# A fused Mamba-2 and quantised-FFN block on one core: new hand-written orders of VectorE, ScalarE, GpSimd and SyncE in the 16-chunk scan

## The reference, cut to what matters

```
x = x + 0.5 * ffn(layernorm(x))          # ffn: 4-bit weights dequantised, 512x512, plus LoRA and bias
h = layernorm(x)
a = h + mamba2(rmsnorm(h, ln1_w))        # 4 heads of 128, state 128x128 each, chunks of 128 tokens
a = a + down(silu(gate(rmsnorm(a, ln2_w))) * up(...))        # inner size 1792
x = x + a
x = x + 0.5 * ffn(layernorm(x))
```

```
z, xs, Bs, Cs, dt = split(h @ w_in.T)         # 512, 128, 128, 512, 4 columns
xs, Bs, Cs = silu(conv4(xs, Bs, Cs));  dt = softplus(dt + dt_bias)
Y  = (tril(exp(cs_q - cs_k)) * (C B^T)) (dt x) + exp(cs) C S_prev + D x
S  = exp(cs_last) S_prev + sum(dec_end * B * dt x)
out = (Y * silu(z)) @ w_out.T
```

## Time and profile before

| what | value |
|---|---|
| median of 3 runs | 782.08 us (781.28 to 782.09) |
| profiled execution, its own time | 783.73 us |
| its span in the trace | 782.0 us |
| PE / DVE / ACT / POOL busy | 96% / 82% / 59% / 45% of the span |
| mean granted PE clock | 0.985 of full |

### The profile page before, as it was taken

One profiled execution on the slowest core, in us unless ns is written; L12 is line 12 of the kernel. 1 busy time (PEld: TensorE's weight loads), 2 busy tenths in 40 slices (PEclk: granted clock), 3 DMA queues, 4 the chain that ended last, 5 costly groups with the idle time before them and its releaser, 6 DMA issues.

```text
span 782.0 us, 10656 instructions
## 1 busy us (share of the span) xinstructions
PE 748.5 (96%) x3424; PEld 364.4 (47%) x3424; DVE 642.9 (82%) x1245; ACT 458.2 (59%) x895; POOL 352.8 (45%) x403
## 2 busy tenths in 40 slices
PE   8999997999899789799999999999999999999998
PEld 3444554555455445354444444444444444444444
DVE  7799998778768887996799988878779779657994
ACT  4868877587765666554536555645645555535451
POOL 5631646565453358866614125124224224223574
PEclk9999999999899899999999999999999999999999
DMA  8934645654421121524060554544544643444464
GB/s 299 186 74 80 167 95 105 138 114 90 83 64 41 41 55 40 128 48 95 14 148 15 103 123 79 140 81 81 139 84 75 148 82 68 76 81 66 105 178 142
DMA packets 98790, 77.67 MB, mean 99 GB/s; under 512 B 65600, under 2 KB 73088, under 8 KB 98736
## 3 DMA queue, kind: packets, MB, share of 16 engines
q0 software_dynamic: 17280, 31.46, 22.6%
q1 hardware_dynamic: 78592, 41.01, 19.9%
q10 hardware_dynamic: 2864, 4.52, 2.4%
HBM read 24.77 MB, written 5.54 MB: 39 GB/s over the span
## 4 chain that ended last, share of the span: by engine, by line
PE 63%; DVE 21%; ACT 8%; issue 4%; DMA 2%; POOL 2%; ACTq 0%; SPq 0%; DVEq 0%; POOLq 0%
PE PS L2123 57%; DVE raw L1578 3%; DVE stage L1578 2%; PE PS L2261 1%; DVE w_in L1682 1%; DVE state L1560 1%; DVE st L1399 1%; DMA x_t<-hb 1%; PE PS L2229 1%; PE PS L2253 1%; DVE h2n_p L1490 1%; DVE xs L1498 1%; ACT xds L922 1%; ACT pre L972 1%; DVE S L1534 1%
## 5 line engine op out<-in xcount | busy, mean ns | idle before, releaser
L2123 PE MATMUL PS<-h,w_in 128*128 128x512 f16 x480 | 111.5, 388 | 0.6 <-DMA h<-hn_p 0.5
L2123 PE MATMUL PS<-h,x_t 128*128 128x512 f16 x408 | 94.0, 379 | 1.7 <-DVE pre L1948 1.6
L773 POOL DMA_DIRECT2D xs<-x x42 | 36.4, 866 | 94.0 <-ACT x L1263 93.1
L2123 PEld LDWEIGHTS PS<-h,w_in 128*128 128x128 f16 x480 | 47.3, 100 | 65.4 <-issue 15.7
L2123 PE MATMUL PS<-n_T,stage 128*128 128x512 f16 x288 | 71.5, 379 | 0.0
L1263 ACT ACTIVATE x<-PS,d_d 128x512 f32<-128x512 f32 x59 | 40.3, 683 | 39.5 <-PE PS L2123 38.6
L2123 PEld LDWEIGHTS PS<-h,x_t 128*128 128x128 f16 x408 | 39.4, 98 | 50.2 <-issue 2.6
L576 POOL TENSOR_TENSOR r<-mv,mhalf 128x1 f32<-128x1 f32 (+1 forms) x32 | 29.4, 920 | 69.3 <-DVE mv L1403 53.0
L2123 PE MATMUL PS<-pre,stage 128*128 128x512 f16 x192 | 49.3, 379 | 0.0
L1233 ACT ACTIVATE xds<-tm,dgh 128x512 f32<-128x512 f32 x24 | 17.3, 722 | 53.3 <-DVE tm L2047 53.3
L2123 PEld LDWEIGHTS PS<-n_T,stage 128*128 128x128 f16 x288 | 28.2, 98 | 34.0 <-ACT x L1263 0.3
(11 more groups left out here) (352 smaller groups left out, 1910.6 us busy)
## 6 DMA issues: line engine op xcount, KB each, us to landing
xs<-x POOLq DMA_DIRECT2D x58, 256.0 KB, 3.3
xs<-n POOLq DMA_DIRECT2D x21, 256.0 KB, 3.3
xl<-x POOLq DMA_DIRECT2D x17, 256.0 KB, 3.3
x_t<-x_in SPq DMA_DIRECT2D x16, 256.0 KB, 3.1
x_t<-hb POOLq DMA_DIRECT2D x16, 256.0 KB, 3.8
out<-x_t SPq DMA_DIRECT2D x15, 256.0 KB, 2.3
raw_gu<-gate_t SPq DMA_DIRECT2D x7, 512.0 KB, 4.5
raw_gu<-up_t SPq DMA_DIRECT2D x7, 512.0 KB, 6.4
```

The lines of the kernel that those rows point to most:

```text
L773: po.dma_start(end_row(c), d_tmps[d % 3], accum_op=ALU.add).then_inc(s_acc[d % 3], 16)
L2123: ins = pe.matmul(out_, lhs(a, b, k), rhs(a, b, k), start=first and n == 0, stop=last and n == len(todo) - 1)
```

## The change

Four things are changed.

1. In steps 0 to 7 the order inside `step(c)` is altered. On POOL, `low_y(c)` goes ahead of `ln1_chain` and `scan_c` at j = 2. On ACT, `conv` is issued ahead of `hi1` at j = 1, and the second slot is copied out ahead of `square` at all j but 2. On DVE, the first two `cut_decay` go ahead of `lo1`.
2. Steps 8 to 15 leave `step` and are written out by hand for DVE, ACT and POOL (`late_steps`). On DVE, `gate_y`, `advance`, `weights` and `scan1` come ahead of taps, `silu`, `lo2`, weight cuts and low parts of sums; on POOL the sums lie between the scan's operations; on ACT `high_y` and `scan_decay` come early.
3. `low_y` of chunks 11 to 15 is on DVE (before: 11, 12, 13, 15; chunk 14 was on POOL). For these chunks `gate_y` writes y in place into PSUM bank B_YT, ACT's `high_y` and DVE's `low_y` read it from there, and PE's `s2_diag(c)` waits for the low part of chunk c-1 too.
4. On SP `load_pair` is cut into `load_gu` and `load_d`. `load_gu(1)` now waits for the first weight cut alone and is issued in step 14, `load_d(1)` is issued after the transpose of chunk 13's h2 (which waits for `lo2(13)` on DVE).

PE's own list is unchanged but for the wait.

Where y of a chunk lives, and `gate_y` on DVE:

```
-        LO_DVE = (11, 12, 13, 15)
+        LO_DVE = range(2 * CH + 3, NCH)
         def y_of(c):
-            return szs[(c // CH) % 2][:, :, cols], y_lo[(c // CH) % 2][:, :, cols]
+            sz = szs[(c // CH) % 2][:, :, cols]
+            return sz, heads(B_YT) if c in LO_DVE else sz, y_lo[(c // CH) % 2][:, :, cols]
...
             def gate_y(c, j):
-                y = szs[(c // CH) % 2][:, :, cols]
-                ve.scalar_tensor_tensor(y, heads(B_YT), d_ih[:, :], y, ALU.mult, ALU.mult).then_inc(e_y, 1)
+                sz, y, _ = y_of(c)
+                ve.scalar_tensor_tensor(y, heads(B_YT), d_ih[:, :], sz, ALU.mult, ALU.mult).then_inc(e_y, 1)
```

PE's added wait in `s2_diag`, and SP's loads within the loop over c:

```
+                if c - 1 in LO_DVE:
+                    pe.wait_ge(e_y_lo, c)
...
+                if c == 3 * CH + 2:
+                    load_gu(1)
...
                 if c > 3 * CH:
                     t2(c - 1)
+                if c == 3 * CH + 2:
+                    load_d(1)
```

`step` of POOL, and of ACT:

```
             def step(c):
                 a = c + 2 * CH
...
+                if c % CH == 2:
+                    low_y(c)
+                ln1_chain(a, a % CH)
+                scan_c(c + 1, (c + 1) % CH)
+                if c % CH != 2:
+                    low_y(c)
...
+                if j in (1, 2):
                     slot_a(i + 1, SLOTS[j][0])
```

`late_steps` of DVE, chunks 10 and 14 of the eight:

```
+                c = 2 * CH + 2
+                gate_y(c, 2)
+                advance(c, 2)
+                bound_row(0)
+                taps(3, 4, 12)
+                for k in range(15, 18):
+                    softplus(3, k)
+                weights(c + 1, 3)
+                scan1(c + 1, 3)
+                silu(3, 4)
+                scale_read(0)
+                lo2(c - 1)
...
+                c = 3 * CH + 2
+                gate_y(c, 2)
+                advance(c, 2)
+                low_y(c)
+                scan1(c + 1, 3)
+                lo2(c - 1)
+                bound_g(1, 0)
+                gate_up(0, 2)
+                residual2(c, 2)
```

More of the change, by code:

```diff
@@ new lines, in step, with late_steps @@
+                if j != 2:
+                    residual2(c, j)
+                slot_b(i + 1, SLOTS[j][0])
+            def late_steps():
+                c = 2 * CH
+                silu_z(2, 3)
+                gate_y(c, 0)
+                advance(c, 0)
+                lo2(c - 1)
+                weights(c + 1, 1)
+                scan1(c + 1, 1)
+                maximum_gu(0)
+                taps(3, 0)
+                softplus(3, 0)
+                softplus(3, 1)
+                softplus(3, 2)
+                residual2(c, 0)
+                silu(3, 0)
+                c = 2 * CH + 1
+                taps(3, 1, 3)
+                gate_y(c, 1)
+                advance(c, 1)
+                weights(c + 1, 2)
+                scan1(c + 1, 2)
+                taps(3, 2, 6)
+                silu(3, 1)
+                silu(3, 2)
+                lo2(c - 1)
+                maximum_gu(1).then_inc(e_max, 1)
+                taps(3, 3, 9)
+                residual2(c, 1)
+                silu(3, 3)
+                c = 2 * CH + 2
+                gate_y(c, 2)
[5 more added lines that the diff above has]
+                weights(c + 1, 3)
+                scan1(c + 1, 3)
+                silu(3, 4)
+                scale_read(0)
+                lo2(c - 1)
+                for k in range(4):
+                    cut_decay(3, k)
+                residual2(c, 2)
+                taps(3, 5)
+                silu(3, 5)
+                c = 2 * CH + 3
+                gate_y(c, 3)
+                scales(0)
+                descale(0)
+                silu_z(3, 0)
+                low_y(c)
+                silu_z(3, 1)
+                advance(c, 3)
+                weights(c + 1, 0)
+                scan1(c + 1, 0)
+                cut_a()
+                lo2(c - 1)
+                silu_z(3, 2)
+                residual2(c, 3)
+                silu_z(3, 3)
+                c = 3 * CH
+                gate_y(c, 0)
+                advance(c, 0)
+                low_y(c)
+                weights(c + 1, 1)
+                scan1(c + 1, 1)
+                lo2(c - 1)
+                t_los(0, 0, 1)
+                gate_up(0, 0)
+                residual2(c, 0)
+                t_los(0, 2)
+                cut_b_gu()
+                c = 3 * CH + 1
+                gate_y(c, 1)
+                advance(c, 1)
+                low_y(c)
+                weights(c + 1, 2)
+                scan1(c + 1, 2)
+                gate_lo(0, 0)
+                gate_up(0, 1)
+                residual2(c, 1)
+                lo2(c - 1)
+                dn_lo(0)
+                t_los(0, 3)
+                gate_lo(0, 1)
+                c = 3 * CH + 2
+                gate_y(c, 2)
+                advance(c, 2)
+                low_y(c)
+                scan1(c + 1, 3)
+                lo2(c - 1)
+                bound_g(1, 0)
+                gate_up(0, 2)
+                residual2(c, 2)
+                bound_g(1, 1)
+                gate_lo(0, 2)
+                bounds(1)
+                c = 3 * CH + 3
+                gate_y(c, 3)
+                low_y(c)
+                t_los(1, 0, 1)
+                lo2(c - 1)
+                gate_up(0, 3)
+                residual2(c, 3)
+                t_los(1, 2, 3)
+                gate_lo(0, 3)
+                bound_row(1)
@@ L1956, in _ @@
             prologue()
[L1957 removed]
+            for c in range(2 * CH):
                 step(c)
+            late_steps()
             lo2(NCH - 1)
```

364 lines of the change are left out of this document (194 added, 170 removed).

## The result

The changed kernel takes 764.79 us (median of 4 runs, 763.31 to 765.24), the one before 782.09 beside it: ratio 0.977, 95% interval 0.974 to 0.980. The forecast was 760.7 us, range 751 to 770. The profiled execution is the fastest of the four, 763.31 us, with a span of 761.6 us.

The account below looks back on a forecast made before the run. The prediction took PE, busy for 96% of the span, as the bound, with only its waits and lost clock to gain. Gains of 12.2 + 9.2 = 21.4 us against the median of 782.08 gave 760.7 us, range 751 to 770.

Parts of the forecast that it names:

- All that can be gained is PE's waits and the clock behind them, 35.1 us.: PE in the scan: ten waits, 24.8 us, plus 10.3 us of lowered clock behind them, are all that can go.
- Steps 0 to 7: 12.2 us.: Early steps: 13.7 us of PE's waits and clock removed, 1.5 given back, so 12.2 us gained.
- Next late: `residual2`, 1.5 us at the ffn product.: Step 2: PE comes 1.3 us before DVE's `residual2` frees the ffn product's bank; 1.5 us given back with semaphores.
- Chunk 10: 3.7 us as 1.4 + 0.9 + 1.4, no clock.: Chunk 10: new PE waits at `bound_spread` (1.4), the decays (0.9) and the bank `scale_read` frees (1.4), 3.7 us.
- Low parts from PSUM 0.68 us.: Chunks 11 to 15: DVE's low part of y takes 0.68 us each from PSUM, 3.4 us for five, beside `gate_up`.
- The load: DVE waits 5.7 us, PE 5.1.: Step 14: DVE waits 5.7 us at `bound_g(1, 0)` for the moved load, PE 5.1 us before `gate_up(0, 3)`.
- That wait I had put at 1.1 us and one chunk later.: Late scan: POOL's sums between its scan operations leave `scan_d(15)` about 1.1 us late, a new PE wait.
- End of the scan 2.4 us.: Step 15: PE waits 2.4 us before its fifth MLP product, behind DVE's low parts, sums and `gate_up(0, 3)`.
- 9.2 for the late steps: Steps 8 to 15: 21.5 us of waits and clock removed less 12.3 us of new waits, 9.2 us gained.
- that the load is hidden: Rival, step 14 and chunk 10: load hidden, small waits smaller; 755.6 us, or 751.9 without the 3.7 too; chance 0.17.
- That DVE and POOL hinder each other: Rival, steps 12 to 15: DVE's SBUF-only instructions beside POOL's sums lose all late gain, 9.2 us, 769.9 us; chance 0.17.
- The slower one, decay before taps: Rival, late steps: `scan1(c+1)` heading DVE's list waits for ACT's decay; 2.7 us a step eats the gain; chance 0.04.

Follow-up runs that it names:

- early_only: The kernel before with only the new orders of steps 0 to 7: 771.75 us, ratio 0.986.
- load_ahead: The changed kernel with the load of raw_d issued ahead of the transpose of chunk 13's h2 instead of behind it: 760.66 us, ratio 0.972.
- late_only: The changed kernel with the orders of steps 0 to 7 put back as before: 776.59 us, ratio 0.991.
- y_in_sbuf: The changed kernel with y of chunks 11 to 15 written to SBUF as before, orders unchanged: 766.59 us, ratio 0.979.
- low10: The changed kernel with `bound_row(0)` ahead of step 9's `residual2` and chunk 10's low part of y on DVE, from PSUM: 763.99 us, ratio 0.975.
- lowy_first: The kernel before with one edit, POOL making the low part of y first in steps 2 and 6: 778.30 us, ratio 0.993.
- load_sums: `load_ahead` with POOL's sums 10 and 11 behind chunk 14's scores, and 14 and 15 behind chunk 15's: 761.46 us, ratio 0.973.

## Why the prediction was right, and where it was not

The sum was 21.4 us of a span of 782.0; the trace gives 20.4, of which 19.3 belong to the change. The medians differ by 17.3, since the profiled execution of before lies 1.6 us above the median beside it and that of after 1.5 below. Point by point:

- *All that can be gained is PE's waits and the clock behind them, 35.1 us.* Held. What was left of it is 11.4 us in waits of over 0.5 us and 4.9 of clock.
- *Steps 0 to 7: 12.2 us.* 12.0 alone by the medians, but 10.3 by the marker in the changed kernel and 10.0 in `early_only`, so some 2 us too much. And the terms were wrong. "Removed: 1.06 + 3.70 + 0.62 + 3.69 + 1.7 + 2.9" credits each edit with the wait that it stood behind. Alone the low part brought 5 us, not the 12.0 of its four terms less the 1.5 given back, and `conv` with the rest in place 4 to 6, not 1.7. The low part itself did as forecast: it starts at 125.00 behind ACT's high part and PE doesn't wait.
- *Next late: `residual2`, 1.5 us at the ffn product.* Wrong place, about the right size: PE waits 0.91 us at the decay rows of step 2, which it reaches earlier and for which DVE is late, since `lo1` (1.47 us) and the statistics stand between the cuts; then 0.57 before a later ffn product and 0.99 at chunk 8's scores.
- *Chunk 10: 3.7 us as 1.4 + 0.9 + 1.4, no clock.* One wait of 3.89 us and 1.7 of clock: 5.6. The step that failed is "It ended this block at ... near 260.4, and then has `gate_y`, `advance` and `bound_row` (2.2 us)": `bound_row` took 2.41 + 0.27 us itself. I had used the mutual hold for large operations alone, and had not laid POOL's list beside DVE's there. The clock behind the wait I had put at nothing.
- *Low parts from PSUM 0.68 us.* Five of five, 0.68 to 0.69.
- *The load: DVE waits 5.7 us, PE 5.1.* DVE 5.15, PE 2.90 plus 1.5 of clock. The mechanism is shown by `load_ahead` (4.1 us back). The clock was charged in full, though I had argued that DVE would be the later one: 2.90 + 1.5 is what the stretch from the `w` of step 14 to the next got shorter by. PE's share was smaller because PE came later: the wait of 2.10 us at chunk 14 and its 1.7 of clock lie just before. That wait I had put at 1.1 us and one chunk later.
- *End of the scan 2.4 us.* None there; PE had lost 3.8 us at chunk 14, where I had 1.1, so DVE was ready.

Late new waits came to 8.9 us and 4.9 of clock, 13.8 where I had 12.3. That the sums are so near is luck: the waits were put 3.4 us too high, and the clock, 4.9 us, at nothing. That 9.2 for the late steps meets the 9.1 of this trace is partly luck too, since the same orders gain 7.3 in `late_only`. By my sum the late gain would be 21.5 - 13.8 = 7.7 us; the markers give 9.1. From the marker of step 8 to the end PE idles 6.8 us less and is busy for 2.3 less, of which the windows' clock explains 0.8; the rest, 1.5 us of PE's busy time, I have not traced to instructions.

The rivals: that the load is hidden was wrong. That DVE and POOL hinder each other was right as a mechanism (2.41, 2.08, and 3.32 us for a pair of weight cuts that took 1.78 in step 11), but it did not take the late gain, and no run here gives its price. The slower one, decay before taps, did not come: DVE's three waits for Ld in the late steps were 0.61 to 0.87 us, far from 2.7.

## What to carry to other kernels

A wait in a trace is what is left after the others: when two engines are both nearly late, price an edit by when its engine would be done if the other waits were gone, and expect the edits together to give their sum only if all of them are made. When a load is moved in a queue, list what it now stands behind and what stands behind its reader; one load in the wrong place cost 4 us here, a quarter of the gain. A DVE operation with all its inputs in SBUF that meets a POOL operation can last until that one ends, and at some places until the next one ends, however small it is; look for such small ones on PE's path, and put one that reads PSUM there if you can. And before you believe a gain of 1 to 2 us, look at the clock behind the waits, which made as much difference between two traces of the same place.

## What the runs showed of the hardware

An operation of 3x3 elements took 2.41 us beside two POOL operations and 0.22 without them; one of 128x4, 2.08 and 0.15; a tap 3.43 and 0.75. The first two ended 0.03 and 0.02 us after the second POOL operation, the tap 0.56 after it, so DVE did not get in between them.

That is not so of every two POOL operations in a row. In step 2 of the kernel before, the weights (L1525) lasted 0.60 us and ended 0.03 after the first, though the second had begun:

```profile
132.11 0.60 DVE L1525 TENSOR_TENSOR wv<-Ld,dt 128x4 f32<-128x4 f32 x1
131.41 1.27 POOL L602 TENSOR_TENSOR stage<-stage,ecs 128x512 f32<-128x512 f32 x1
132.65 1.27 POOL L607 TENSOR_TENSOR stage_r<-stage,split 128x512 fp32r<-128x512 f32 x1
```

In step 10 of that kernel a tap ended 0.55 us after the first of two (266.44, 1.68 us), and there the second POOL operation took 1.70 us instead of 1.27. Over all traces, among taps, weights, `mdg` and the low parts of `y_in_sbuf`, I count 14 holds over two POOL operations. In all 14 the two stand right behind the DMA issue of `rms2` (L627 here; the first starts 0.7 us after it), and the second starts some 0.3 us before the recorded end of the first; where the hold ended with the first of two, they did not stand there. Why that place differs stays open.

The Trainium skill (SBUF — State Buffer, Who interferes with whom) says that one blocks the other for the whole instruction. Most holds in the traces agree, over one POOL operation; the 14 show more. That y in PSUM escapes it is shown by L1668 (0.68 against up to 2.94 us).

The clock is not settled by the length of the last wait. Behind waits of 2.10 us (changed kernel), 2.12 (`low10`) and 2.21 (`lowy_first`) the next 10 us show 0.83, but 1.00 behind 2.40 (`load_sums`), 2.95 (`early_only`, shown here) and 3.01 (`low10`, at 320.68):

```profile
282.50:292.50 10.00, 10.00 (x44) 5.53 (x45) 5.68 (x14) 8.49 (x20) 7.17 (x8) 1.00 0.27 55
```

My rule from the earlier trace rows, that waits from 2.9 us on cost it and those up to 1.6 us don't, was two groups of a few cases. What decides between 2.1 and 3 us stays open, and so does why 3.9 us at one and the same place cost 1.7 us in some traces and up to 3.1 in others.
